# A state-space scan whose B and C rows come through DRAM, and which begins with one batch element while the other's step sizes follow inside it

## The reference, cut to what matters

```python
xz = x @ W_in.T;  x_val, z = jnp.split(xz, 2, axis=-1)          # 512 channels each
xv = conv1d(x_val, conv_w, 4 taps) + conv_b;  x_val = silu(xv)
A = -jnp.exp(A_log)                                              # 512 x 16
dt = jax.nn.softplus(x[:, :, :64] @ W_dt.T + b_dt)
Bm = x @ W_B.T;  Cm = x @ W_C.T                                  # 16 numbers per token each
# for every token t:
dA = jnp.exp(dt_t[:, :, None] * A[None])
h = dA * h + (dt_t * xv_t)[:, :, None] * B_t[:, None, :]
y_t = jnp.einsum('bdn,bn->bd', h, C_t)
y = y * silu(z);  out = y @ W_out.T
```

## Time and profile before

| what | value |
|---|---|
| median of 3 runs | 2669.26 us (2663.39 to 2670.34) |
| profiled execution: its own time | 2667.91 us |
| its span in the profile | 2666.0 us |
| busy share: PE, DVE, ACT, POOL | 79%, 78%, 49%, 45% |
| granted TensorE clock, mean | 0.921 of full speed |

### The profile page before, as it was taken

The page is one execution under the profiler, slowest core; times in us unless marked ns, Lnnn a source line. Parts: engine busy times, 40 slices in busy tenths (PEclk is TensorE's granted clock), DMA queues, the critical chain, the costliest instruction groups (busy, mean ns, idle before and its releaser), DMA issues.

```text
span 2666.0 us, 24454 instructions
## 1 busy us (share of the span) xinstructions
PE 2102.9 (79%) x8572; PEld 1148.4 (43%) x8572; DVE 2076.5 (78%) x2425; ACT 1314.5 (49%) x1874; POOL 1212.8 (45%) x567
## 2 busy tenths in 40 slices
PE   2998877778799886777779898677878988867786
PEld 0326652236433764223542476322453256632254
DVE  5865869996785578997778467899688748789957
ACT  0564366554165436664417544565343744455623
POOL 1211259991221116997222110899521212289932
PEclk9999888889899988999889998799989999989998
DMA  5200000000220000000032000000003100000000
GB/s 179 87 13 0 1 0 0 0 0 1 68 84 1 1 1 0 0 0 0 1 101 51 1 1 0 0 0 0 0 1 115 37 1 1 0 0 0 0 1 16
DMA packets 41072, 51.26 MB, mean 19 GB/s; under 512 B 9072, under 2 KB 32368, under 8 KB 40944
## 3 DMA queue, kind: packets, MB, share of 16 engines
q1 hardware_dynamic: 40944, 49.62, 5.9%
HBM read 26.25 MB, written 10.49 MB: 14 GB/s over the span
## 4 chain that ended last, share of the span: by engine, by line
PE 46%; DVE 25%; POOL 14%; ACT 6%; issue 6%; DMA 1%; SPq 0%; POOLq 0%; DVEq 0%; ACTq 0%
PE psum L678 14%; PE psum L944 12%; POOL big L1798 10%; PE psum L807 5%; POOL big L1787 4%; ACT big L1022 3%; PE psum L743 3%; PE psum L795 3%; PE psum L780 3%; DVE mid L1602 3%; ACT mid L1022 2%; DVE mid L1320 2%; DVE mid L1248 2%; DVE negmax L1430 2%; PE psum L814 2%
## 5 line engine op out<-in xcount | busy, mean ns | idle before, releaser
L944 PE MATMUL psum<-big,ident 128*128 128x512 f32 x992 | 528.1, 682 | 202.5 <-POOL big L1798 202.1
L1668 DVE TENSOR_TENSOR_SCAN big<-psum,b,big 128x512 f32<-128x512 f32 x512 | 614.3, 1263 | 0.0
L1798 POOL TENSOR_TENSOR big<-big 128x2048 f32<-128x2048 f32 x124 | 559.8, 4514 | 22.2 <-DVE big L1668 22.2
L1022 ACT ACTIVATE big<-psum 128x1024 f32<-128x1024 f32 (+2 forms) x592 | 448.7, 776 | 243.1 <-PE psum L795 143.5
L1022 ACT ACTIVATE psum<-mid,aneg 128x512 f32<-128x512 f32 x512 | 353.9, 692 | 265.0 <-DVE big L1668 265.0
L944 PEld LDWEIGHTS psum<-big,ident 128*128 128x128 f32 x992 | 203.7, 216 | 485.5 <-POOL big L1798 264.7
L1430 DVE TENSOR_REDUCE negmax<-psum 128x1 f32<-128x512 f32 x512 | 318.8, 678 | 48.9 <-PE psum L780 47.8
L1787 POOL TENSOR_TENSOR big<-mid,big 128x512 f32<-128x512 f32 (+1 forms) x128 | 222.7, 1740 | 19.9 <-ACT big L1022 19.9
L780 PE MATMUL psum<-mid 96*128 96x512 bf16 x512 | 189.7, 391 | 34.4 <-DMA mid<-mid 23.5
L795 PE MATMUL psum<-mid 98*128 98x512 bf16 x512 | 181.8, 382 | 20.1 <-ACT big L1022 14.2
L1022 ACT ACTIVATE mid<-mid 128x513 f32<-128x513 f32 (+3 forms) x120 | 102.9, 881 | 191.2 <-DVE mid L1301 190.7
(11 more groups left out here) (199 smaller groups left out, 3427.1 us busy)
## 6 DMA issues: line engine op xcount, KB each, us to landing
mid<-mid SPq DMA_DIRECT2D x192, 64.0 KB, 2.6
mid<-scratch SPq DMA_DIRECT2D x192, 64.0 KB, 2.2
scratch<-big SPq DMA_DIRECT2D x4, 1536.0 KB, 6.1
out<-hres SPq DMA_DIRECT2D x8, 513.0 KB, 5.9
big<-in_x SPq DMA_DIRECT2D x8, 512.0 KB, 4.6
big<-in_w SPq DMA_DIRECT2D x2, 1024.0 KB, 6.4
big<-in_wg SPq DMA_DIRECT2D x1, 1024.0 KB, 9.7
big<-in_wu SPq DMA_DIRECT2D x1, 1024.0 KB, 11.7
```

The source lines that it names most:

```text
L944: mm = nc.tensor.matmul(y_psum[:, c], ident[:, :], st(1, k)[:, c], start=(n == 0), stop=(n == NS - 1))
L1022: return nc.scalar.activation(o, a, func, **kw)
L1668: V.tensor_tensor_scan(st(0, k)[:, c], a_psum(DT * k + c), st(0, k)[:, c], b0[:, p, n, c:c + 1], ALU.mult, ALU.add).then_inc(scanned, 1)
L1798: G.tensor_tensor(st(1, k), st(0, k), c_row(k).unsqueeze(1).broadcast_to([P, DT, S]), ALU.mult).then_inc(hc_ready, 1)
```

## The change

1. **Rows through DRAM.** B and C are computed once in fp32 on 32 partitions (`wbc` is 32 columns wide instead of 96). VectorE copies them to SBUF (`copy_bc`), SyncE stores them to DRAM (`bc_dram`), and for each step reads row B and row C back onto all 128 partitions, into four buffers each (`b_row`, `c_row`, ROWS = 4). GpSimdE takes both rows from there. ScalarE's 64 copies of rows and TensorE's spreads of C are gone.
2. **fp32 spreads.** TensorE still spreads row B for VectorE, now by an fp32 matmul from the identity, two steps ahead; it waits for VectorE's own reading (`b_used`) instead of ScalarE's copy.
3. **Late z.** The gates' inputs of batch 1 are computed inside the scan, one tile at each of steps 3, 6, 9, 12 (`late_z`), copied by ScalarE a step later (`z_raw`), and passed through silu after the last exponential. Only their token 0 is done ahead of the scan (`z_first`).
4. **Batch 0 alone.** The order ahead of the scan puts batch 0 first (`MAMBA_FILLS`). Batch 1's step sizes (`steps_of(1)`), its product with x (`times_x`, on VectorE now instead of GpSimdE), and its token 0 (`token0(1)`) are VectorE instructions in steps 4, 7 and 10 of the scan (`LATE_STEPS`).

The tables that set the order:

```diff
+MAMBA_FILLS = [(f"d{c}", 0) for c in range(DT)] + [("x0", 0), ("x1", 0)] + [(f"d{c}", 1) for c in range(DT)] \
+    + [("x2", 0), ("x3", 0), ("bc", 0), ("bc", 1), ("x0", 1), ("x1", 1)] + [(f"z{c}", 0) for c in range(DT)] \
+    + [("x2", 1), ("x3", 1)]
...
+Z_STEPS = (3, 6, 9, 12)
...
+LATE_STEPS = (4, 7, 10)
+ROWS = 4
```

SyncE's new rows:

```diff
+                for p in range(PAIR):
+                    sp.wait_ge(bc_copied, p + 1)
+                    sp.dma_start(bc_dram[p], bc_rows(p)).then_inc(bc_stored[p], 16)
+                for k in range(PAIR * NS):
+                    p, n = divmod(k, NS)
...
+                    if k >= ROWS:
+                        sp.wait_ge(b_pool, k - ROWS + 1)
+                    sp.dma_start(b_row(k), bc_dram[p, n:n + 1, 1:T].broadcast_to([P, S])).then_inc(b_in[k % ROWS], 16)
+                    if k >= ROWS:
+                        sp.wait_ge(hc_ready, k - ROWS + 1)
+                    sp.dma_start(c_row(k), bc_dram[p, NS + n:NS + n + 1, 1:T].broadcast_to([P, S])).then_inc(
+                        c_in[k % ROWS], 16)
```

TensorE in the scan:

```diff
                 def spread_b(k):
+
                     if k:
-                        pe.wait_ge(b_copied, k)
-                    spread_row(k, k % NS, b_psum).then_inc(b_spread, 1)
...
+                        pe.wait_ge(b_used, k)
+                    r = k % NS
+                    nc.tensor.matmul(b_psum, ident[0:2 * NS, r:r + 1].broadcast_to([2 * NS, P]),
+                                     bc_rows(k // NS)[:, 1:T], start=True, stop=True).then_inc(b_spread, 1)
...
                     if k + 2 < PAIR * NS:
                         spread_b(k + 2)
-                    if k + 1 < PAIR * NS:
-                        spread_c(k + 1)
                     if k:
                         add_y(k - 1)
+                    if k in Z_STEPS:
+                        late_z(Z_STEPS.index(k))
```

ScalarE in the scan:

```diff
-                            if c == 1:
-                                if k >= 2:
-                                    act.wait_ge(hc_ready, k - 1)
-                                act.wait_ge(c_spread, k + 1)
-                                run(c_row(k), c_psum, ACT.Copy).then_inc(c_copied, 1)
-                                if k + 1 < PAIR * NS:
-                                    copy_b(k + 1)
+                            if c == 2 and k - 1 in Z_STEPS:
+                                zc = Z_STEPS.index(k - 1)
+                                act.wait_ge(z_full, zc + 1)
+                                run(mid4(1, 1)[:, zc, 1:T], z_psum, ACT.Copy).then_inc(z_raw, 1)
```

VectorE ahead of the scan, and what it has to do in step k of the scan, between the product for step k+1 and the four scan instructions:

```diff
+                taps(0, 0)
+                taps(0, 1)
+                round_up(0)
+                taps(0, 2)
+                taps(0, 3)
+                for p in range(PAIR):
+                    copy_bc(p)
+                round_up(1)
+                steps_of(0)
+                for c in range(DT):
+                    taps(1, c)
+                first_sums()
...
+                    if k == LATE_STEPS[0]:
+                        steps_of(1)
+                    if k == LATE_STEPS[1]:
+                        times_x()
+                    if k == LATE_STEPS[2]:
+                        token0(1)
```

More of the change, by code:

```diff
@@ L130, in plan_fills @@
     ln(3)
[L131 to L134, removed]
+    while len(order) % 4:
+        order.append(None)
+    order.extend(MAMBA_FILLS)
     while len(order) % 4 != 2:
@@ L910, in turn_products @@
[L910 to L919, removed]
@@ L921, in spread_row, with mamba_input @@
-                def spread_row(k, r, o):
-                    return nc.tensor.matmul(o, sel[:, r:r + 1].broadcast_to([96, P]), bcp[:, k // NS, 1:T],
-                                            start=True, stop=True)
+                def mamba_input(name, p):
+                    kind, c = name[0], int(name[-1]) if name != "bc" else 0
+                    if kind == "d":
+                        fill(name, p, [(wdt[:, c * P:(c + 1) * P], big_un(p)[:, 0])])
+                    elif kind == "b":
+                        fill(name, p, [(wbc[:, k], big_un(p)[:, k]) for k in range(KT)], rows=2 * NS)
+                    else:
+                        wt = wx if kind == "x" else wz
+                        fill(name, p, [(wt[:, k, c * P:(c + 1) * P], big_un(p)[:, k]) for k in range(KT)])
@@ L934, in spread_c, with late_z @@
+                def late_z(c):
+                    if c:
+                        pe.wait_ge(z_raw, c)
                     else:
                         pe.wait_ge(first_copied, 1)
-                    spread_row(k, NS + k % NS, c_psum).then_inc(c_spread, 1)
+                        pe.wait_ge(z_first, 1)
+                    for k in range(KT):
+                        mm = nc.tensor.matmul(z_psum, wz[:, k, c * P:(c + 1) * P], big_un(1)[:, k, 1:T],
+                                              start=(k == 0), stop=(k == KT - 1))
+                    mm.then_inc(z_full, 1)
@@ new lines, in _, with silu_z @@
+                absolute(0)
+                first_tap(0, 0)
+                first_tap(0, 1)
+                exponential(0)
+                for c in range(DT):
+                    step_input(1, c)
+                logarithm(0)
+                first_tap(0, 2)
+                absolute(1)
+                first_tap(0, 3)
+                exponential(1)
+                first_tap(1, 0)
+                logarithm(1)
+                nc.scalar.preload_act_table(ACT.Silu)
+                def silu_z(c):
@@ L1189, in _ @@
[L1189 to L1200 removed]
+                first_tap(1, 1)
@@ new lines, in _ @@
+                silu(0, 0)
+                silu(0, 1)
+                silu_z(0)
+                silu(0, 2)
+                silu_z(1)
+                silu(0, 3)
+                silu_z(2)
+                silu_z(3)
+                silu(1, 0)
+                first_tap(1, 2)
+                silu(1, 1)
+                first_tap(1, 3)
+                act.wait_ge(first_full, 1)
+                run(mid4(1, 1)[:, :, 0], z_psum[:, 2 * PAIR * NS:2 * PAIR * NS + DT], ACT.Silu).then_inc(z_first, 1)
@@ L1605, in _, with round_up, taps @@
-                for p in range(PAIR):
+                def round_up(p):
+                    dve.wait_ge(sp_act, 3 * p + 2)
+                    affine2(big4(p, 1), mid4(p, 3), 1.0, 1.0, ALU.add, ALU.subtract).then_inc(sp_round, 1)
+                def taps(p, c):
+                    k = DT * p + c
+                    dve.wait_ge(m_tap0, k + 1)
+                    xp, acc = slot(f"x{c}", p), mid4(p, 0)[:, c]
+                    for n in range(1, 4):
+                        if n > 1:
+                            dve.wait_ge(m_tap, 3 * k + n - 1)
+                        V.scalar_tensor_tensor(out=acc[:, n:T], in0=xp[:, 0:T - n], scalar=col("mw", 4 * c + 3 - n),
+                                               in1=acc[:, n:T], op0=ALU.mult, op1=ALU.add).then_inc(m_tap, 1)
```

251 lines of the change are left out of this document (120 added, 131 removed).

## The result

| | before | after |
|---|---|---|
| median | 2667.01 us (4 runs, 2663.39 to 2670.34) | 2718.19 us (4 runs, 2713.77 to 2720.64) |
| ratio | 1 | 1.019 [1.017, 1.0211] |
| profiled execution, its span | 2667.91, 2666.0 | 2713.77, 2712.0 |

A forecast was written before the change was run, and what follows sets the result against it. VectorE and GpSimdE, nearly equally full in the scan, were taken as the bound. Terms of -4.2 + 6.1 + 6.0 + 6.1 + 0.9 - 0.9 gave 14.0 us a turn, 56 in all: 2724 us, range 2702 to 2746.

The forecast's parts named there:

- Start of the scan: From the first d tile to scan 0: batch 0 going first starts the scan 4.2 us earlier a turn.
- Step sizes: Scan step 4: batch 1's VectorE instruction waits 3.7 us for GpSimdE, then runs 2.4; 6.1 us a turn.
- Product with x: Scan step 7: VectorE's instruction takes 2.2 us behind a 3.8 wait for GpSimdE; 6.0 us a turn.
- Token 0: Scan step 10: two tiny VectorE instructions, a 3.7 us wait, GpSimdE's 2.2 us product between them; 6.1 us a turn.
- Late z: ScalarE's z copies in the scan: VectorE's stalls cover all but step 13's; 0.9 us a turn.
- Gate of batch 0: Gate of batch 0: its 1.80 us wait shrinks as GpSimdE no longer lags; 0.9 us less a turn.
- fp32 spreads, rows through DRAM, ScalarE's copies: In the scan: spreads covered by TensorE's idle time, row reads hidden, removed copies worth nothing; 0 each.
- The tail: From the last scan instruction to the first tail gate: no change forecast, 0 us.
- no stalls: In the scan, two-input VectorE instructions run beside GpSimdE and pay only their length; 2659 us, chance 9%.
- half absorbed: In the scan, stalls come but partly replace time lost anyway; 6 us a turn, about 2692 us, chance 8%.
- TensorE the bound: In the scan, slower sums plus fp32 spreads make TensorE exceed the step; 2780 us, chance 6%.
- GpSimdE first every time: At the three late places, VectorE also waits for GpSimdE's next product; 18 to 19 us a turn, 2741, chance 9%.

The follow-up runs named there:

- asked first: Kernel after, with the late VectorE instructions moved ahead of VectorE's product, right behind the scans, and token 0's second one in step 11: 2676.81 us, ratio 1.0044.
- all ahead: Kernel after, with batch 1's step sizes, product with x and token 0 put ahead of the scan again: 2687.36 us, ratio 1.0092.
- control: Kernel after, with batch 1's step sizes in step 5 instead of 4 and its product with x in step 8 instead of 7: 2729.38 us, ratio 1.0247.
- The two-buffer kernel: Kernel after, with two buffers instead of four for each of the rows B and C: 2715.62 us, ratio 1.0183.
- The other order of the start: Kernel after, with product 0 ahead of token 0's small instructions, these reading B from PSUM, and batch 0's gate of token 0 in step 2: 2696.21 us.

## Why the prediction was right

Its working, term by term (us a turn):

- *Start of the scan*, -4.2, measured -4.7. The order of events was as told: from the first d tile, GpSimdE's product with x was forecast at +29.3 and ran at +29.7 (1037.51); product 0 at +46.8, ran at +45.4; scan 0 at +51.2, ran at +50.5. Two GpSimdE instructions of the softplus took 3.82 each, not the 4.55 counted; that is 1.5. Against it, product 1 followed product 0 after 3.9 us, not 3.3.
- *Step sizes*, +6.1, measured 5.80 (1082.67 to 1088.47). *Product with x*, +6.0, measured 5.93. *Token 0*, +6.1, measured 5.9 from 1130.97 to the end of L1736. In turn 1 it was the other way round, 5.77 and 0.21: GpSimdE's short product went in ahead of the first and not between the two. The sum is the same, but the order told in the prediction failed there.
- *Late z*, +0.9: 3.8 / 4 = 0.95. The number holds only because stalls cover three of the four copies, as the prediction said. Where stalls cover fewer of them or none, the runs show 2.8 (asked first), 4.6 (all ahead) and 5.2 (control).
- *Gate of batch 0*, -0.9: 1.05 of waiting in turn 2 where there had been 1.80, so -0.75; over the four turns 1.24 against 1.81, so -0.6.
- *fp32 spreads, rows through DRAM, ScalarE's copies*: 0 each. The two-buffer kernel supports it for the rows; for the spreads it is read from the waits, 2 us inside all four scans, 0.5 a turn; the kernel with all of it ahead bounds the three together at 0.6.
- *The tail* was counted at nothing and gave 1.1. Most of this is luck, by TensorE's clock, which the prediction did not look at here. The eight matmuls of the last whole sum, of turn 2 before and of the kernel after:

```profile
1246.64 5.28 PE L944 MATMUL psum<-big,ident 128*128 128x512 f32 x8 [2.90 <-POOL big L1798]
...
1273.41 3.70 PE L997 MATMUL psum<-big,ident 128*128 128x512 f32 x8 [2.90 <-POOL big L1891]
```

Before they took 5.2 to 5.4 us in all four turns, at a granted clock of 0.69 of full speed in turn 2; in turns 2 and 4 of the kernel after they took 3.70, at 1.00. That is 0.8 in the mean. The other 0.3 is that this sum began 1.1 us after the last scan instruction in place of 1.4.

So the terms are right to about 1 us each, with misses on both sides: 0.5 less at the start, 0.6 less in the three stalls, 1.1 less in the tail, 0.3 more at the gate, 0.5 more for the spreads. Together they make 12.6 of the forecast 14.0, where 12.8 was read.

Of the rivals, *no stalls* fell with L1670 at 5.88; *half absorbed* with the second half of the scan, which gave back 1 us, not 6; *TensorE the bound* with sums of 532 us, 4.29 for eight instructions; *GpSimdE first every time* with L1670, behind which GpSimdE's next product waited; it happened once, to L1733 in turn 1. The second rival's own sum was off: 14.0 less the 4.1 of head start that it adds and less 0.9 to 1.8 at the gate leaves 8 to 9 a turn, 2700 to 2704, not 6 and 2692. The forecast does not hang on it. That the order of asking decides was read before from three places; the kernel that asks first makes it a cause and not only a pattern, with the one exception shown above.

What the prediction had no eye for: that the wait of the tiny instructions ahead of the scan could be avoided. It counted it, and took it as given. The other order of the start is worth 6 us a turn, more than the change's own head start.

## What to carry to other kernels

When GpSimdE is near full, an extra VectorE instruction with two SBUF inputs costs its place in the queue, not its length (5.9 us for 2.3, 2.2 for a 128x4). Put it right behind the link that frees VectorE while GpSimdE is in a short instruction, or take one input from PSUM, and look for tiny instructions with such durations first. Time freed on an engine that is not waited for was worth nothing here, and a wait that is taken away is worth only the distance to the next engine in line.

## What the runs showed of the hardware that was not expected

- GpSimdE's 128x2052 subtraction and addition of the softplus took 3.82 us each for batch 1 and 4.55 for batch 0, in the kernel after and in every variant (1041.99 and 1045.96 against 1020.66 and 1025.36 in turn 2); before, none took less than 4.55. VectorE's taps do not explain it: they ran beside the first of the short ones (1043.24 to 1047.79), but beside a long one, too (1023.87 to 1028.66). The cause is open.
- A read of one 2 KB row of DRAM onto 128 partitions (256 KB) landed in 3.7 us, where a 64 KB transfer takes 2.2: four times the bytes for 1.7 times the time.
